# One chunk of table rows in 48 fetched row by row by SyncE and ScalarE instead of by GpSimd's indirect transfer

## The reference

```
deg = clip(segment_sum(ones, src, n), 1)          # out-degree
h = feats * rsqrt(deg)[:, None]                   # the "table", 6250 rows of 256 floats
m = segment_sum(h[src], dst, n) * rsqrt(deg_in)   # one table row of 1 KB for every edge
gc = m @ W_gc + b_gc;  x = gc + (feats @ W_res + b_res)
logits = x @ Wg + bg                              # top 2 of 64 experts, then the experts,
                                                  # batch norm, residual and layer norm
```

## Time and profile before

| | |
|---|---|
| median of 3 runs | 2977.45 us (2967.4, 2977.45, 2977.49) |
| the profiled execution's own time | 2967.47 us |
| its span, first to last instruction | 2965.7 us |
| busy in the span | PE 2067.3, POOL 1885.7, DVE 1235.3, ACT 410.3 us |
| mean granted clock of TensorE | 0.833 of full speed |

### The profile page before, as it was taken

One profiled execution on the slowest core, in us unless ns is written; L12 is line 12 of the kernel. 1 busy time (PEld: TensorE's weight loads), 2 busy tenths in 40 slices (PEclk: granted clock), 3 DMA queues, 4 the chain that ended last, 5 costly groups with the idle time before them and its releaser, 6 DMA issues.

```text
span 2965.7 us, 44135 instructions
## 1 busy us (share of the span) xinstructions
PE 2067.3 (70%) x10204; PEld 1712.2 (58%) x10251; DVE 1235.3 (42%) x3115; ACT 410.3 (14%) x1358; POOL 1885.7 (64%) x1969
## 2 busy tenths in 40 slices
PE   8956556566665666666767776777758898999670
PEld 7944444454444545555555565656647788888650
DVE  8971212223223333444445445555562222222267
ACT  3010000000000001010111111111112222232213
POOL 0017777777777777777777777777725677777500
PEclk6557777777878888888989989999978899999885
DMA  8033333333333333333333333333324456666532
GB/s 295 0 102 107 106 106 106 106 107 108 108 107 108 110 107 110 110 109 109 111 110 111 109 112 111 111 111 113 111 70 121 140 182 198 196 192 186 169 124 87
DMA packets 205082, 362.76 MB, mean 122 GB/s; under 512 B 43080, under 2 KB 125814, under 8 KB 204814
## 3 DMA queue, kind: packets, MB, share of 16 engines
q0 software_dynamic: 93648, 230.69, 26.9%
q1 hardware_dynamic: 104058, 123.31, 13.1%
q10 hardware_dynamic: 7108, 6.43, 0.6%
HBM read 327.91 MB, written 57.52 MB: 130 GB/s over the span
## 4 chain that ended last, share of the span: by engine, by line
POOL 33%; PE 28%; issue 18%; DVE 8%; DMA 6%; DVEq 4%; ACT 1%; PEld 1%; POOLq 1%; ACTq 1%; SPq 0%; PEldq 0%
POOL ring L456 16%; POOL stage L456 16%; PE bank L1264 7%; PE bank L1148 7%; PE bank L1258 5%; DMA ring<-nodes,slots 3%; PE bank L1128 3%; PE bank L1189 2%; PE bank L1249 1%; PE bank L1168 1%; DMA stage<-y 1%; DVE stage L744 1%; DMA ring<-table,ring_idx 1%; DVE slots L844 1%; DVE acc L1046 1%
## 5 line engine op out<-in xcount | busy, mean ns | idle before, releaser
L456 POOL DMA_INDIRECT ring<-table,ring_idx x792 | 749.3, 946 | 241.9 <-issue 240.4
L456 POOL DMA_INDIRECT stage<-table,ring_idx x771 | 729.1, 946 | 234.7 <-issue 231.5
L1148 PE MATMUL bank<-ring,hot 128*128 128x257 f32 x1056 | 305.2, 452 | 163.1 <-DMA ring<-table,ring_idx 153.9
L1148 PE MATMUL bank<-stage 128*128 128x257 f32 x1030 | 304.1, 459 | 135.4 <-DMA stage<-table,ring_idx 126.0
L1148 PEld LDWEIGHTS bank<-ring,hot 128*128 128x128 f32 x1056 | 237.3, 231 | 224.9 <-issue 142.1
L1148 PEld LDWEIGHTS bank<-stage 128*128 128x128 f32 x1030 | 236.3, 235 | 197.5 <-issue 101.1
L940 DVE TENSOR_TENSOR acc<-acc,bank 128x257 f32 x196 | 82.9, 423 | 560.7 <-PE bank L1148 523.9
L480 POOL DMA_INDIRECT ring<-nodes,slots x192 | 200.7, 1045 | 93.0 <-issue 58.9
L490 POOL DMA_INDIRECT y<-ring,slots x192 | 198.3, 1033 | 90.3 <-issue 55.6
L1258 PEld LDWEIGHTS bank<-ring,stage 128*128 128x128 f32 x1984 | 239.0, 198 | 11.7 <-issue 6.6
L1258 PE MATMUL bank<-ring,stage 128*128 128x128 f32 x1984 | 241.5, 281 | 4.1 <-issue 1.7
(11 more groups left out here) (226 smaller groups left out, 2478.1 us busy)
## 6 DMA issues: line engine op xcount, KB each, us to landing
stage<-in_L_gnn_w_dram SPq DMA_DIRECT2D x128, 512.0 KB
ring<-table,ring_idx POOLq DMA_INDIRECT x792
y<-zeros SPq DMA_DIRECT2D x49, 256.0 KB, 2.1
stage<-y SPq DMA_DIRECT2D x14, 896.0 KB, 7.1
stage<-table,ring_idx POOLq DMA_INDIRECT x771
stage<-in_L_gnn_b_dram SPq DMA_DIRECT2D x64, 128.0 KB
nodes<-yS ACTq DMA_DIRECT2D x49, 128.0 KB
xs<-in_x_dram SPq DMA_DIRECT2D x1, 6144.0 KB
```

The source lines that it names most:

```text
L456: pool.indirect_dma_start(out=ring(q)[:, j, 0:D], out_offset=None, in_=table[:, :], in_offset=bass.IndirectOffsetOnAxis(ap=ring_idx[:, q, ...
L1148: last = pe.matmul(bank[:, 0:D + 1], hots[:, j, :], ring(q)[:, j, :], start=j == 0, stop=j == n - 1)
```

## The change

In each of the 32 full steps the last chunk of slot 5 (`ROW_Q` = 5) is no longer gathered by POOL. SP loads the chunk's 128 source numbers from HBM into one partition of `rng` (`row_list`). SP then takes rows 0 to 95 in three blocks: one TENSOR_LOAD fills 32 registers, and 32 plain DMAs each fetch one table row of 1 KB, at the address that a register gives, into one partition of the new buffer `row_buf`. ACT does the same for rows 96 to 127 in four turns of 8, one turn after its work for each of the slots 0 to 3. After its work for slot 4, ACT waits for all 128 rows and copies `row_buf` into the ring's last chunk of slot 5. PE waits for that copy before slot 5. SP may begin the next step's rows when the copy is done (`rows_placed`), and reload the list when ACT has read its part (`list_read`).

```
+ROW_Q = RING - 1
+BLOCK = 32
+SP_BLOCKS = 3
+ACT_ROWS = 8
...
+        def row_of(eng, reg):
+            node = nc.s_assert_within(eng.snap(reg), 0, N - 1,
+                                      skip_runtime_bounds_check_because="the list of sources holds nodes")
+            return table[bass.ds(node, 1), :]
...
+            def list_rows(it):
+                at = it * (RING * CPG * P) + (ROW_Q * CPG + CPG - 1) * P
+                sp.dma_start(row_list, src[bass.ds(at, P)].rearrange("(o e) -> o e", o=1)).then_inc(listed, 16)
+            def fetch_rows(it):
+                sp.wait_ge(listed, it * 16 + 16)
+                sp.sem_inc(sp_starts, 1)
+                for b in range(SP_BLOCKS):
+                    sp.load(row_regs, row_list[0:1, b * BLOCK:(b + 1) * BLOCK])
+                    for r in range(BLOCK):
+                        sp.dma_start(row_home(b * BLOCK + r), row_of(sp, row_regs[r])).then_inc(rows_sp[b], 16)
...
+            with sp.Fori(1, STEPS - 1) as it:
+                sp.wait_ge(list_read, it)
+                list_rows(it)
+                sp.wait_ge(rows_placed, it)
+                fetch_rows(it)
...
-                    for j in range(LASTJ if final and q == LASTQ - 1 else CPG):
+                    for j in range(pool_chunks(q, final)):
...
+            def fetch_rows(it, turn, first):
...
+                act.load(row_regs, row_list[0:1, r0:r0 + ACT_ROWS])
+                for r in range(ACT_ROWS):
+                    act.dma_start(row_home(r0 + r), row_of(act, row_regs[r])).then_inc(rows_act, 16)
+                if turn == ACT_TURNS - 1:
+                    act.sem_inc(list_read, 1)
+            def place_rows(it, first):
...
+                    act.wait_ge(acc_added, it * RING)
+                for b in range(SP_BLOCKS):
+                    act.wait_ge(rows_sp[b], it * (16 * BLOCK) + 16 * BLOCK)
+                by_act = 16 * ACT_ROWS * ACT_TURNS
+                act.wait_ge(rows_act, it * by_act + by_act)
+                act.sem_inc(act_starts, 1)
+                act.activation(ring(ROW_Q)[:, CPG - 1, 0:D], row_buf[:, :], ACT.Copy).then_inc(rows_placed, 1)
...
                     ticks_of_group(act, group_code(act, it * RING + q), tick)
+                    if q < ACT_TURNS:
+                        fetch_rows(it, q, first)
+                    elif q == ROW_Q - 1:
+                        place_rows(it, first)
...
+                    if q == ROW_Q and not final:
+                        pe.wait_ge(rows_placed, it + 1)
```

More of the change, by code:

```diff
@@ L119, in graph_moe_kernel @@
         code = sb("code", [1, GCOLS], I32)
+        row_list = rng[0:1, 0, 0:P].bitcast(I32)
+        row_buf = sb("row_buf", [P, D])
         deg = sb("deg", [P, NT])
@@ L220, in graph_moe_kernel @@
         code_ready = sem("code_ready")
+        listed, list_read, sp_starts = sem("listed"), sem("list_read"), sem("sp_starts")
+        rows_placed = sem("rows_placed")
+        rows_sp, rows_act = [sem(f"rows_sp{b}") for b in range(SP_BLOCKS)], sem("rows_act")
         idx_ready = sem("idx_ready")
@@ L272, in ring, with row_home, pool_chunks @@
             return ring_low[:, q, :, :] if q < RING // 2 else ring_high[:, q - RING // 2, :, :]
+        def row_of(eng, reg):
+            node = nc.s_assert_within(eng.snap(reg), 0, N - 1,
+                                      skip_runtime_bounds_check_because="the list of sources holds nodes")
+            return table[bass.ds(node, 1), :]
+        def row_home(r):
+            return row_buf[r:r + 1, :]
+        def pool_chunks(q, final):
+            if final:
+                return LASTJ if q == LASTQ - 1 else CPG
+            return CPG - 1 if q == ROW_Q else CPG
         iota_ps = banks[5][:, 3 * P:4 * P]
@@ L380, in weights @@
                 sp.dma_start(b2s[:, par, :], b2[bass.ds(e, 1), :].rearrange("o d -> (o d)").partition_broadcast(P)).then_inc(b2_in[par], 16)
+            row_regs = [sp.alloc_register(f"sp_row{r}") for r in range(BLOCK)]
+            def list_rows(it):
[8 more added lines that the diff above has]
+                        sp.dma_start(row_home(b * BLOCK + r), row_of(sp, row_regs[r])).then_inc(rows_sp[b], 16)
+            sp.wait_ge(code_ready, 1)
+            sp.wait_ge(nb_done, 1)
+            list_rows(0)
+            sp.wait_ge(table_first, 16)
+            sp.wait_ge(table_rest, 16 * (NB - 1))
+            fetch_rows(0)
+            with sp.Fori(1, STEPS - 1) as it:
[3 more added lines that the diff above has]
+                fetch_rows(it)
             sp.wait_ge(slots_mm, 1)
@@ L575, in indices @@
                 if not first:
-                    act.wait_ge(gath[q], it * (16 * CPG))
+                    act.wait_ge(gath[q], it * (16 * pool_chunks(q, False)))
                 act.activation(ring_idx[:, q, :], srcT[:, bass.ds((it * RING + q) * CPG, CPG)], ACT.Copy).then_inc(idx_ready, 1)
@@ L614, in _ @@
             act.wait_ge(code_ready, 1)
+            row_regs = [act.alloc_register(f"act_row{r}") for r in range(ACT_ROWS)]
+            ACT_TURNS = (P - SP_BLOCKS * BLOCK) // ACT_ROWS
+            def fetch_rows(it, turn, first):
+                r0 = SP_BLOCKS * BLOCK + turn * ACT_ROWS
+                if turn == 0:
+                    if first:
+                        act.wait_ge(table_first, 16)
+                        act.wait_ge(table_rest, 16 * (NB - 1))
+                    else:
+                        act.wait_ge(rows_placed, it)
+                    act.wait_ge(listed, it * 16 + 16)
+                    act.sem_inc(act_starts, 1)
[5 more added lines that the diff above has]
+            def place_rows(it, first):
+                if first:
+                    act.wait_ge(code_ready, 1)
+                else:
+                    act.wait_ge(acc_added, it * RING)
[3 more added lines that the diff above has]
+                act.wait_ge(rows_act, it * by_act + by_act)
+                act.sem_inc(act_starts, 1)
+                act.activation(ring(ROW_Q)[:, CPG - 1, 0:D], row_buf[:, :], ACT.Copy).then_inc(rows_placed, 1)
             def step(it, first):
@@ L1219, in step @@
                     n = LASTJ if final and q == LASTQ - 1 else CPG
-                    pe.wait_ge(gath[q], it * (16 * CPG) + 16 * n)
+                    by_pool = 16 * pool_chunks(q, False)
+                    pe.wait_ge(gath[q], it * by_pool + 16 * pool_chunks(q, final))
+                    if q == ROW_Q and not final:
+                        pe.wait_ge(rows_placed, it + 1)
                     if first and q == RING // 2:
```

## The result

The changed kernel takes 3021.17 us (median of 5 runs, 3007.64 to 3025.94), the kernel before 2974.08 us beside it. The ratio is 1.0159, interval 1.014 to 1.0178: 1.6% slower. The forecast was 24 us faster. The range held the time, the direction was wrong, and so the forecast's sum was.

The account below looks back on a forecast made before the run. POOL's gathers were taken to bound the second stage until about 1750 us, then sums and ticks. 31 us gained, less 1 for other waits and 6 for the late copy, made 24 less: 2948 us, range 2930 to 3085.

Parts of the forecast that it names:

- POOL sets the pace to about 1750 us, then the sums and ticks: Second stage: gathers at 1.2505 us bound it until 1749.7; 25 of 32 removed gathers count, 31 us, less 1.
- SP's loop fits if a load of 32 takes under 5.1 us: SP's step: 44.3 us with cheap loads, 67.5 with dear ones, against POOL's 58.8 us; this unknown decides the case.
- the choice of the lower side: SP's loads of 32 registers: forecast took about 0.3 us each, cost mostly paid once, a choice no row shows.
- Neither bound: SP's load of 32 registers: 0.3 us if paid once, 8 us if each register costs 0.25 us.
- The first rival: SP's loop becomes the bound because loads cost by the register: 3041 or 3046 us at 0.20 us each; chance 0.32.
- A row costs 0.42 us: SP's row fetches: 0.24 us DMA plus 0.18 us between DMAs, 0.55 at the other end; 96 rows 40.3 us.
- The fetched rows don't overlap: Third rival, row DMAs: each has its engine until landed, 269 us a step, or partly so, above 3400; chance 0.06.
- all cost in transfers: DMA engines: 256 added packets a step, 15 us of an engine, costed at nothing; gathers land 0 to 1 us late.
- the cost of ACT's turns: ACT's turns of 8 rows, 3.7 to 5.4 us each in four of six groups, costed at nothing.
- The copy behind slot 4: only where slot 4 has a tick, up to 8 us, I take 6: PE's wait before slot 5: 4 us at each slot-4 tick behind 1750 us, two such ticks found.
- what POOL gains after 1750 us is lost: Second stage's end: from 1752.69 the last chain runs through PE, DVE and ACT only, so later POOL gains don't count.

Follow-up runs that it names:

- experiment 1: Changed kernel without the row fetches: slot 5's last chunk is neither gathered nor replaced in the 31 steps after the first; 2920.0 us, ratio 0.983.
- experiment 4: Changed kernel, but POOL gathers all 48 chunks and the copy goes to an unread buffer, PE still waiting for it; 3043.3 us, ratio 1.0258.
- experiment 3: Changed kernel, but after the first step the copy goes to an unread buffer and PE doesn't wait for it; 2922.52 us, ratio 0.9834.
- experiment 2: Changed kernel, but ACT fetches its 32 rows only once, without turns in the steps; SP's rows, copy and PE's wait stay; 2965.86 us, ratio 0.998.
- experiments 5 and 8: Changed kernel with rows fetched a step ahead and the copy behind slot 1 (2945.62 us, ratio 0.9924) or slot 2 (2948.3 us, ratio 0.9918).
- experiment 6: Changed kernel with ACT's 32 rows in two turns of 16 behind slots 0 and 1; 2988.06 us, ratio 1.0064.

## Why the prediction was wrong

- *POOL sets the pace to about 1750 us, then the sums and ticks.* Right, and sized right for POOL's gain: 30 us forecast, 29.6 measured (experiment 1). But what is lost on PE isn't won back from about 1640 us on (the kernel after from group 142, experiment 4 too), 110 us earlier than the point that the prediction used.
- *SP's loop fits if a load of 32 takes under 5.1 us.* Right, and the choice of the lower side was right: 2.12 us. Neither bound held as such. The load grows by about 0.06 us a register ((2.12 - 0.28) / 31, the 0.28 being ACT's), between "paid once" and 0.25. By the figure of the Trainium skill ("Runtime: NRT & Kernel Launch", section "Instruction fetch mechanics"), 0.2 us a register, it would have been about 6.4 us, an estimate; for a list in SBUF the trace does not agree. The first rival gave the right direction for the wrong reason. (Its time at 0.18 us a register doesn't follow from its own formula: P is about 60.8 there, and the time about 2980, not 2991. Nothing rests on it.)
- *A row costs 0.42 us.* Right: 0.423 to 0.425.
- *"The fetched rows don't overlap"* and all cost in transfers: nothing, as taken (experiment 3). SP's queue has 110266 packets instead of 104058. The 6208 more are two for each of 3104 one-partition DMAs (3072 rows and 32 lists), the 256 packets a step that the prediction had counted for 128 rows.
- **The step that failed** is the cost of ACT's turns: "A turn stands behind a tick's last instruction, so it delays only what comes next: numbers that POOL needs about 50 us later, and the next tick. [...] I cost it at nothing." What also comes next is the copy, which the change itself put behind those turns in the same program and for which PE waits. I listed what was queued behind a turn from the program before, not from the changed one. It cost 38.5 us (changed kernel against experiment 2, by the two traces; the medians of their runs, 3021.17 and 2965.86, are 55 us apart).
- *The copy behind slot 4: only where slot 4 has a tick, up to 8 us, I take 6.* The mechanism was right, the term too small: 29.9 us (experiment 2 against 1). Each wait at such a tick was the 4 us forecast, but the count was wrong. I had looked only at ticks in slot 4 and only behind 1750 us, and found two. In experiment 2 there are three that count, and five more waits of 2.1 to 2.3 us where slot 3 has the tick: 24.1 us. The rest comes in slower groups and ticks on PE behind the waits; how much of it each of them has I can't tell.
- *Each of these happens where POOL isn't the bound.* The prediction said that what POOL gains after 1750 us is lost. It didn't draw the other conclusion, that every wait put on PE there counts in full. Experiment 4 shows it: all of its 70.9 us were lost after the sum of group 142.

That PE's wait for the copy is the cause is shown in two ways: with all the added work in place, taking away the wait (experiment 3) gives back the whole gain of the second stage, 29.6 us, and only moving the copy (experiments 5 and 8) gives back 20.1 and 17.0 of it.

## What to carry to other kernels

When work is moved to an idle engine, ask for each instruction that another engine will wait for: what stands ahead of it in that engine's own program, in the kernel as changed, and is the waiting engine ever faster there than on average? A hand-over that is just in time at the average pace is late wherever the receiver works off a backlog. Prepare it a step earlier (here: fetch ahead, copy three slots before it is needed); that turned 1.6% slower into 0.8% faster without taking away any work.

## What the runs showed of the hardware

A wait on PE cost more than its length: from the sum of group 142 on, PE waits 53.0 us for the copy and the kernel falls back by 67.1 us. Behind such a wait the granted clock is lower. The clock of the kernel after in the wait shown above and behind it (us from to, length, PE busy, granted clock, DMA share, GB/s):

```profile
2030.00:2037.00 7.00, 0.00 (x0) 0.63 0.38 109
2037.00:2050.00 13.00, 10.91 (x37) 0.76 0.37 106
```

0.63 and 0.76 are means over the two levels, 1.2 and 2.4 GHz. PE had been idle for 7.5 us, and the next 16 products took 6.14 us instead of 3.75 just before. Over 1750 to 2100 us the mean was 0.93 in the kernel before (first line), and 0.89 in the kernel after (second):

```profile
1750.00:2100.00 350.00, 259.69 (x1129) 0.93 0.39 111
```

```profile
1750.00:2100.00 350.00, 243.00 (x1032) 0.89 0.36 103
```

The clock falls in the kernel before as well, so not every slow group is due to the copy. A load of several registers costs by the register, but little: 0.28 us for one on ACT, 0.557 for 8, 1.032 for 16 (experiment 6), and 2.12 for 32 on SP.
